# A preactivated two-layer attention kernel: the split queries and keys are folded across partitions by direct transfers, and the steps around them are retimed

## The reference, cut to what matters

```python
x = x + _L0_conv_ref(_gn(x), ...)   # 8 heads of 16, attention over all 256 positions, a relative bias
x = x + _L1_conv_ref(_gn(x), ...)   # 16 heads of 16, in chunks of 64 positions

# second layer
qkv = flat @ w_qkv.T
scores = jnp.einsum('bclhd,bcmhd->bchlm', q, k_cat) * scale   # k_cat: chunk i-1 and chunk i
attn = jax.nn.softmax(scores, axis=-1)
out = jnp.einsum('bchlm,bcmhd->bclhd', attn, v_cat)
out = out.reshape(B, T, H * HD) @ w_out.T
```

## Time and profile before

| what | value |
| --- | --- |
| times of three runs | 172.42, 173.70, 179.64 us (median 173.7) |
| the profiled execution's own time, and its span | 175.27 us, 173.4 us |
| TensorE busy, matmuls | 151.1 us (87%) |
| VectorE, ScalarE, POOL busy | 111.1, 107.9, 53.0 us |
| share of the span on the chain that ended last | PE 64%, DVE 14%, DMA 6%, issue 6%, ACT 5% |
| first scores of units 4, 5, 6, 7 | 90.1, 108.6, 126.2, 143.2 us |
| end of the transposes of the last block | 162.8 us |

### The profile page before, as it was taken

One profiled execution on the slowest core, in us unless ns is written; L12 is line 12 of the kernel. 1 busy time (PEld: TensorE's weight loads), 2 busy tenths in 40 slices (PEclk: granted clock), 3 DMA queues, 4 the chain that ended last, 5 costly groups with the idle time before them and its releaser, 6 DMA issues.

```text
span 173.4 us, 4284 instructions
## 1 busy us (share of the span) xinstructions
PE 151.1 (87%) x1582; PEld 130.9 (75%) x1582; DVE 111.1 (64%) x326; ACT 107.9 (62%) x218; POOL 53.0 (31%) x106
## 2 busy tenths in 40 slices
PE   7989769849989879999999798999999869989872
PEld 7568649737778578988797678988989758879751
DVE  1544776774366586277629887799687983898220
ACT  1427516857558457946795769775986774856520
POOL 0302540859946225762781122012200200000000
PEclk9999879999999999999999999999999996999999
DMA  6409900000000000049804990199309860100111
GB/s 184 138 4 275 325 6 4 0 0 0 6 2 0 4 0 2 0 121 242 246 4 104 233 266 6 32 243 240 102 5 259 206 202 0 34 14 17 34 55 42
DMA packets 8564, 15.84 MB, mean 91 GB/s; under 512 B 1208, under 2 KB 5688, under 8 KB 7776
## 3 DMA queue, kind: packets, MB, share of 16 engines
q1 hardware_dynamic: 7984, 15.22, 31.8%
q10 hardware_dynamic: 560, 0.35, 0.8%
HBM read 10.31 MB, written 5.26 MB: 90 GB/s over the span
## 4 chain that ended last, share of the span: by engine, by line
PE 64%; DVE 14%; DMA 6%; issue 6%; ACT 5%; POOL 2%; ACTq 1%; SPq 0%; DVEq 0%
PE bank L556 7%; PE bank L590 7%; PE bank L578 6%; PE bank L609 6%; PE bank L669 5%; PE bank L600 4%; PE bank L679 4%; PE bank L716 4%; PE bank L567 4%; DMA K<-k_terms 3%; PE bank L479 3%; DMA PT<-buckets 3%; DVE NM L962 2%; PE bank L712 2%; DVE SB L958 2%
## 5 line engine op out<-in xcount | busy, mean ns | idle before, releaser
L1197 ACT ACTIVATE PT<-bank 128x512 f32<-128x512 f32 x64 | 38.3, 598 | 23.0 <-PE bank L609 12.4
L958 DVE CUSTOM_DVE_ANT_0 SB<-bank,Tk 128x256 f32<-128x256 f32 x64 | 24.4, 420 | 20.6 <-PE bank L578 20.5
L362 POOL TENSOR_SCALAR SB<-SB,NM 128x256 f32<-128x256 f32 x64 | 29.9, 482 | 12.1 <-DVE NM L958 11.7
L962 DVE TENSOR_REDUCE NM<-bank 128x4 f32<-128x512 f32 x32 | 21.9, 685 | 12.7 <-PE bank L590 12.4
L590 PE MATMUL bank<-K,QP 96*128 96x128 f32 x128 | 21.8, 294 | 1.7 <-DMA K<-k_terms 1.7
L969 DVE TENSOR_TENSOR SB<-bank,NM 128x512 f32<-128x512 f32 x32 | 22.1, 692 | 1.1
L578 PE MATMUL bank<-KH,QM 128*128 128x256 f32 x64 | 20.6, 343 | 2.1 <-ACT QM L1177 2.1
L1188 ACT ACTIVATE QP<-Q,con 96x512 fp32r<-96x512 f32 x32 | 21.2, 713 | 0.0
L590 PEld LDWEIGHTS bank<-K,QP 96*128 96x128 f32 x128 | 17.8, 197 | 3.7 <-DMA K<-k_terms 2.0
L609 PE MATMUL bank<-con,SB 128*128 128x128 f32 x128 | 20.4, 283 | 0.0
L600 PE MATMUL bank<-con,SB 128*128 128x128 f32 x128 | 19.3, 273 | 0.0
(11 more groups left out here) (142 smaller groups left out, 269.7 us busy)
## 6 DMA issues: line engine op xcount, KB each, us to landing
q_terms<-WQK SPq DMA_DIRECT2D x16, 128.0 KB, 2.3
k_terms<-KHL SPq DMA_DIRECT2D x16, 128.0 KB, 2.4
Q<-q_terms SPq DMA_DIRECT2D x4, 512.0 KB, 5.4
K<-k_terms SPq DMA_DIRECT2D x4, 512.0 KB, 5.2
Tk<-bias_rows SPq DMA_DIRECT2D x4, 384.0 KB, 4.8
X<-x SPq DMA_DIRECT2D x4, 256.0 KB, 4.2
Q<-q_terms SPq DMA_DIRECT2D x4, 256.0 KB, 5.8
K<-k_terms SPq DMA_DIRECT2D x4, 256.0 KB, 6.1
```

Source lines behind the costliest of these rows:

```text
L362: last = nc.gpsimd.tensor_scalar(rows_of, rows_of, -1.0, NM[:, i % 2, 2 * u + nt:2 * u + nt + 1], ALU.mult, ALU.add)
L958: last = V.tensor_tensor_reduce(SB[:, idx % SRING, nt * CH:(nt + 1) * CH], half, Tk[:, u, nt * P:nt * P + CH], 1.0, LOWEST, ALU.add, ALU.m ...
L962: V.tensor_reduce(NM[:, i % 2, 4 * u:4 * u + 4], s[:].rearrange("p (h m) -> p h m", h=4), AX.X, ALU.max).then_inc(max_ready, 1)
L1197: A.activation(PT[:, u, :], bank[Z_BANK + u % 2][:], ACT.Exp, scale=-SCALE if is_a(i) else SCALE).then_inc(p_ready, 1)
```

## The change

The terms no longer go through DRAM. Each of queries and keys is moved by three transfers of 256 KB, from the 128 partitions of one part of QHL or KHL straight into 32 partitions of Q3 or K3. For that the four groups have to stand interleaved (partition 4r + a instead of 32a + r), which is done once, by writing the columns of the weights in that order: `weights_b` and `low_weights` take two instructions of 256 columns, with a step of four elements at the destination, where they took one of 512 for the first two weight blocks.

The tables change too. GM and GV, QK and V come one step later; XT stays. The half-chains of units 4 to 6 have T1, T2 and out one step earlier, with PV where it was. In the last unit PV is two steps earlier, T1 and T2 three, out three. VA is copied at the end of the step of its transposes and not early in the next step.

```diff
@@ -176,8 +176,6 @@
 
-        q_terms = nc.dram_tensor("q_terms", (BATCH, 2, GRP, PAIRS, 2 * TOK), F32, kind="Internal").ap()
-        k_terms = nc.dram_tensor("k_terms", (BATCH, 2, GRP, PAIRS, 2 * TOK), F32, kind="Internal").ap()
         rows = nc.dram_tensor("bias_rows", (HA, NDIAG), F32, kind="Internal").ap()
@@ -190,7 +188,7 @@
         fills, dve_fills = sem("fills"), sem("dve_fills")
-        q_written, k_written, q_loaded, k_loaded = (sem(n) for n in ("q_written", "k_written", "q_loaded", "k_loaded"))
+        q_loaded, k_loaded = sem("q_loaded"), sem("k_loaded")
         spread_ready = sem("spread_ready")
@@ -227,6 +225,9 @@
 
+        def pair_columns(w, n, k):
+            return w[:, k, n * CH:(n + 1) * CH].rearrange("p (g r a) -> p g a r", g=2, a=PAIRS)
+
         def grouped(t, b):
@@ -243,12 +244,12 @@
         TIMES_A = [(range(1, 2), (-6, -4, -5, -5)), (range(2, 3), (-5, -3, -4, -4)), (range(3, BATCH), (-9, -7, -8, -8))]
-        XT_B, GM_B, GV_B, QK_B, V_B = -14, -13, -12, -9, -7
+        XT_B, GM_B, GV_B, QK_B, V_B = -14, -12, -11, -8, -6
 
...
         FINISH = [(IN_A, (9, 12), (13, 13), (14, 14), (16, 16)),
-                  (range(BATCH, UNITS - 1), (10, 13), (12, 15), (14, 17), (16, 19)),
-                  (range(UNITS - 1, UNITS), (10, 13), (12, 15), (13, 16), (14, 17))]
+                  (range(BATCH, UNITS - 1), (10, 13), (11, 14), (13, 16), (15, 18)),
+                  (range(UNITS - 1, UNITS), (8, 11), (9, 12), (10, 13), (11, 14))]
 
@@ -283,29 +284,23 @@
 
-            def put_terms(b, terms, hl, ready, written):
-
-                sp.wait_ge(ready, BATCH + b + 1)
-                for a in range(PAIRS):
-                    sp.dma_start(terms[b, :, :, a, :].rearrange("s p n -> p s n"), hl[a * GRP:(a + 1) * GRP].bitcast(F32)).then_inc(written, 16)
-
-            def get_terms(b, terms, dst, both, high, written, loaded):
-
-                sp.wait_ge(written, 16 * PAIRS * (b + 1))
-                sp.dma_start(dst[GRP * both:GRP * (both + 2)], terms[b].rearrange("s p a n -> (s p) (a n)")).then_inc(loaded, 16)
-                sp.dma_start(dst[GRP * high:GRP * (high + 1)], terms[b, 0].rearrange("p a n -> p (a n)")).then_inc(loaded, 16)
+            def fold_terms(b, hl, parts, dst, loaded):
+
+                for s, part in enumerate(parts):
+                    sp.dma_start(dst[GRP * s:GRP * (s + 1), b % 2].rearrange("p a g n -> p a (g n)").bitcast(F32),
+                                 hl[:, part, :].bitcast(F32)).then_inc(loaded, 16)
 
...
 
-                n, i = b % 2, BATCH + b
-                put_terms(b, q_terms, QHL, q_ready, q_written)
-                put_terms(b, k_terms, KHL, k_ready, k_written)
+                i = BATCH + b
+                sp.wait_ge(q_ready, i + 1)
                 if b >= 2:
                     sp.wait_ge(qp_ready, NCH * (b - 1))
-                get_terms(b, q_terms, Q3[:, n].rearrange("p a g n -> p (a g n)"), 0, 2, q_written, q_loaded)
+                fold_terms(b, QHL, (0, 1, 0), Q3, q_loaded)
+                sp.wait_ge(k_ready, i + 1)
                 if b >= 2:
                     sp.wait_ge(s_done, BLK * (i - 1))
-                get_terms(b, k_terms, K3[:, n].rearrange("p a g n -> p (a g n)").bitcast(F32), 1, 0, k_written, k_loaded)
+                fold_terms(b, KHL, (0, 0, 1), K3, k_loaded)
 
@@ -621,7 +616,7 @@
                 elif u == 0:
-                    pe.wait_ge(k_loaded, 32 * (i - BATCH + 1))
+                    pe.wait_ge(k_loaded, 16 * TERMS * (i - BATCH + 1))
                 if not is_a(i) and u % 2 == 0:
@@ -901,8 +896,13 @@
                 src = bank[O_BANK][:].rearrange("p (k r) -> p k r", k=2)
-                V.tensor_tensor(WTl[:, :, n * CH:(n + 1) * CH], src, WTh[:, :, n * CH:(n + 1) * CH].bitcast(F32),
-                                op=ALU.subtract).then_inc(wl_ready, 1)
+                if n < 2:
+                    for k in range(CT):
+                        last = V.tensor_tensor(pair_columns(WTl, n, k), src[:, k].rearrange("p (g a r) -> p g a r", g=2, a=PAIRS),
+                                               pair_columns(WTh, n, k).bitcast(F32), op=ALU.subtract)
+                else:
+                    last = V.tensor_tensor(WTl[:, :, n * CH:(n + 1) * CH], src, WTh[:, :, n * CH:(n + 1) * CH].bitcast(F32), op=ALU.subtract)
+                last.then_inc(wl_ready, 1)
 
@@ -1032,9 +1032,6 @@
                     norm_x(2, t - 6)
-                for units, when in TIMES_A:
-                    for i in due(t, when[3] + 1, units):
-                        value_rows(i)
                 for step, when in enumerate((XT_B, GM_B, GV_B, GV_B + 1)):
@@ -1049,6 +1046,9 @@
                             queries_keys(i, which)
+                for units, when in TIMES_A:
+                    for i in due(t, when[3], units):
+                        value_rows(i)
                 for units, pv, t1, t2, out_step in FINISH:
@@ -1099,8 +1099,12 @@
                 src = bank[O_BANK][:].rearrange("p (k r) -> p k r", k=2)
-                dst = WTh[:, :, n * CH:(n + 1) * CH] if n < 3 else WoT[:]
-                A.activation(dst, src, ACT.Copy).then_inc(wb_ready, 1)
+                if n < 2:
+                    for k in range(CT):
+                        last = A.activation(pair_columns(WTh, n, k), src[:, k].rearrange("p (g a r) -> p g a r", g=2, a=PAIRS), ACT.Copy)
+                else:
+                    last = A.activation(WTh[:, :, n * CH:(n + 1) * CH] if n == 2 else WoT[:], src, ACT.Copy)
+                last.then_inc(wb_ready, 1)
 
@@ -1136,12 +1140,12 @@
                         if b:
-                            act.wait_ge(q_written, 16 * PAIRS * b)
+                            act.wait_ge(q_loaded, 16 * TERMS * b)
                         A.activation(QHL[:, 0, :], f[:], ACT.Copy).then_inc(qh_ready, 1)
...
                         if b:
-                            act.wait_ge(k_written, 16 * PAIRS * b)
+                            act.wait_ge(k_loaded, 16 * TERMS * b)
                         A.activation(KHL[:, 0, :], f[:], ACT.Copy).then_inc(kh_ready, 1)
@@ -1181,7 +1185,7 @@
                 if c == 0:
-                    act.wait_ge(q_loaded, 32 * (b + 1))
+                    act.wait_ge(q_loaded, 16 * TERMS * (b + 1))
                 if b * NCH + c >= QRING:
...
                 for v in range(2):
```

## The result

The change made the kernel slower: 200.59 us median (199.67 to 202.11) against 175.45 for the kernel before on the same chip, a ratio of 1.160, 95% interval 1.145 to 1.175. I had forecast 173.5, range 168.8 to 177.5. The profiled execution has a span of 200.3 us.

A forecast was written before the change was run, and what follows sets the result against it. TensorE, busy 151.1 of 173.4 us, was taken to bound the kernel through its waits. Gains of 8.6 less costs of 8.4 left 0.2 faster: 173.7 - 0.2 = 173.5 us, range 168.8 to 177.5.

The forecast's parts named there:

- Will the fold be in time?: Second layer's direct transfers of queries and keys: taken to land in 10 us, between 8.5 and an upper bound of 11.5.
- The windows: Time from a unit's first transfer issue until TensorE wants the keys: 11, 12, 14 at units 4 to 6, 10.8 at 7.
- The fold is too slow: Slower rival: scores of units 4 to 7 wait for late keys; at 14 us transfers, 183.4 us in all; chance 0.07.
- The new waits bring the clock down: Slower rival: clock falls behind waits of XT, V or GV, 1.7 each; one or two falls 0.18, three or more 0.10.
- The keys' wait and its clock: Unit 7's first scores: the wait for the keys' transfer (1.7) and the low clock behind it (1.7) go, 3.4 gained.
- VA's wait: First layer's query products no longer wait for VA's copy to free bank 7: 1.7 us gained.
- Y's 2.0: PV's three waits for the residual of the unit before go because out is a step earlier: 2.0 us gained.
- GM's waits: GM one step later: 0.9 of waiting for unit 3's queries and about 0.6 for copied values go, 1.5 gained.
- The tables' costs: Later waits on TensorE's path: XT and V 4.6, GV 0.7, QK 1.2, the scores 1.2, the last unit 0.4.
- QP's spread: Scores at units 4 and 5 wait for ScalarE's query spread, 0.8 and 0.4: 1.2 cost, between nothing and 2.6.
- wait of QK for XTl: QK's last part waits 0.4, three times, for ScalarE's low part of the normalised input: 1.2 us cost.
- The split of the weights: Weight copies by halves delay TensorE's wait for QM: 0.3 us cost, bounds 0.2 and 2.4 with halves at 0.60 each.

The follow-up runs named there:

- after_shift: The changed kernel with 156 more instructions, waits on an already reached semaphore, in TensorE's program ahead of the opening's moments: 208.75 us, ratio 1.196.
- tables_only: The kernel before with the new tables and VA's copy moved, keeping transfers through DRAM and whole weights: 183.53 us, ratio 1.023 to the kernel before.
- quad: The changed kernel with the six transfers sent to every fourth partition, the fourth rows filled once and masked: 176.84 us, against 178.12 for the kernel before.
- quad_old_tables: quad with all tables of the kernel before: 173.37 us, ratio 0.978 to the kernel before.
- best_old: quad_old_tables measured again in a later side-by-side comparison: 173.83 us, ratio 0.988 to the kernel before.
- probe: The kernel before plus eight transfer groups behind its end, engines still: three transfers into 32 neighbouring partitions took 8.3 us, to every fourth 3.8.
- probe2: The kernel before plus seven transfer groups behind its end, engines still: six into 32 neighbouring partitions took 14.7 us, six to every fourth 5.8.
- probe3: The kernel before plus six transfer groups behind its end, including exchanged partition halves: median packets 84 ns both ways to every fourth partition.

## Why the prediction was wrong, step by step

**The step that failed** is "Will the fold be in time?". I took 10 us for 1.57 MB, between two rates that both had DRAM at one end, and called 11.5 the upper bound. It is 14.6, or 108 GB/s. I wrote myself that nothing of that kind was in the trace, and still used the nearest rows as if they were bounds. The 6.1 us were a read from DRAM; it gives no upper limit for a transfer whose source lies in SBUF too. The six folds took the same 14.7 us with all engines still and 5.8 to every fourth partition, so what I had wrong is the rate into 32 partitions and not the work beside it. The nearest row is not a bound: what is not measured can lie beyond it.

**The windows were right.** The keys were wanted at 90.28 - 3.52 - 75.60 = 11.2 us behind the first issue at unit 4 (forecast 11), 11.0 at unit 5 (12), in after_shift 174.32 - 3.17 - 159.67 = 11.5 at unit 7 (10.8), and none late at unit 6 (14).

**"The fold is too slow"** had 0.07 and was the case that came. At 14 us I had it as waits of 3, 2, 0 and 3.2 and a time of 183.4. The waits at units 4 and 5 were 3.5 and 3.7. Unit 7, which I had at 3.2, was held up by the stalls and did not wait. The 17 us more are in the main two things that I had not priced: the stalls of TensorE for its instructions, 7.7, and the clock, which fell behind each of the four stops of 3.5 us or more, where I had priced one fall. Summed over the four windows of low clock above, (1 - clock) times length is 3.0 + 3.2 + 3.1 + 3.4 = 12.7 us, so over 3 a fall and not the 1.7 of before; the fall behind XT adds 1.7. That is 7.7 + 12.7 + 1.7 less the 1.7 priced and less the 1.0 of waits that did not come, 19.4; part of the low clock lies in the stops themselves and counts twice.

**The skill's rule on ports.** The Trainium skill, "SBUF — State Buffer", Door 1, gives 189 GB/s for 1 MiB into 32 partitions. No run here moves 1 MiB into 32 partitions in one transfer, so the figure itself is not tested. As a rate for six folds in a row it was no bound: they took 108 GB/s with all fixed times and 127 from the first packet to the last, and the measurement decides. One fold by itself had its packets in 1.4 us, 186 GB/s, but was 67 GB/s from issue to the end of the wait.

**"The new waits bring the clock down"** had 0.18 for one or two falls and came true once: behind unit 7's XT, which waited 1.98 us, the clock was at 0.50 for 3.4 us, which is 1.7 us of work. It did so in tables_only and after_shift too. But in quad the same XT waits 1.99 us and the clock stays at 1.00, so the length of the wait alone does not decide it; what does is open.

**The gains.** The keys' wait and its clock, 3.4, less 0.3 for the weights, is 3.1: quad_old_tables was 3.9 us faster (2.2%, between 1.1 and 3.3%), best_old 2.1 (1.2%, 0.2 to 2.2%). Both agree with it. VA's wait is gone (1.7, right). Of Y's 2.0 a wait of 0.9 is left in the last unit. Of GM's waits (0.9 and 1.6, of which I counted 1.2) 1.5 were to go, and 1.2 went: 1.3 are left.

**The tables' costs.** I had 8.4 less 0.3, against 5.2 of gains by tables: 2.9 slower. By the medians quad is 3.5 slower than quad_old_tables. In the changed kernel XT waited 2.0 and 0.8 (forecast 2.2, 1.2, and 0.6 at unit 5, where it did not wait); GV 0.8 (1.0); V 0.8 (1.0); the last T1 0.7 (0.75). QP's spread cost 0.8 at unit 7 and not at units 4 and 5, where the keys covered it; in quad it is 0.9 in two waits. No wait of QK for XTl is among the rows, so those 1.2 were wrong.

**The split of the weights.** ScalarE's row for it:

```profile
L1104 ACT ACTIVATE WTh<-bank x4: 647/662/687, 28.5 to 32.0; 128x256 fp32r<-128x256 f32 x4
```

A half at a step of 16 bytes takes 0.66 us, more than the 0.60 of the whole 512 columns before, so even my upper bound for the instruction was too low. The note on cachelines in the Trainium skill, "SBUF — State Buffer" (Door 1), has each access in a new line pay, and the trace agrees in direction: 256 columns took 0.66 at a step of 16 bytes and 0.51 without. On the path it cost little, but not where I looked. TensorE's waits for QM are 2.2 us where they were 2.1 in all. The new wait is for VectorE's low part, at the transposes of the next weights:

```profile
PE bank L728 <- DVE WTl L901: 0.8, 1, 0.8
```

Every kernel with the strided weights has it, with 0.8 or 0.3 us, and none that writes whole blocks. By these rows the split cost TensorE 0.4 to 0.9 us where I took 0.3, and at another place.

## What to carry to other kernels

A transfer of a form that the trace does not hold should be measured alone before a kernel is built on it, in the number in which it will be queued: from the first packet to the last, one fold here ran at 186 GB/s and six in a row at 127. When the rows go to few partitions, try spreading them over all 128 first; a contraction does not care which partitions its rows lie in. And two edits that each cost 2 or 3% can cost 16 together when one makes shorter the window that the other needs longer.

## What the runs showed of the hardware

- TensorE's program comes in packets of 16 KB that the profile counts among those of the DMA engines. In the changed kernel two of them, at 137.7 and 162.5 us, came while a fold ran, and TensorE stopped for 4.0 and 3.7 us in the middle of a group of products; the profile calls it "issue". It depends on the place in the program: with 156 more instructions ahead (after_shift) both stops were gone.
- Packets of 2 KB took 84 to 87 ns to every fourth partition (quad, probe, probe2, probe3) and in a single fold, and 267 to 288 in folds in a row, in the kernel (median 282 to 288 at units 4 to 6) as with all engines still. Into 64 partitions of one half it was 258 to 265.
- An instruction of TensorE that only waits for a value already there took 106 ns from one start to the next when many stood in a row (after_shift).
- Strided writes of 256 columns at 16 bytes: 0.66 us on ScalarE against 0.60 for 512 contiguous ones, 0.62 on VectorE against 0.69.
- Behind an XT that waited 1.98 us the granted clock fell to 0.50 in the changed kernel, tables_only and after_shift; behind one of 1.99 in quad it stayed at 1.00.
